# Softmax weights in five chunks of 128 rows in place of six of 122, with bias and condition moved out of the matmul

## The chip, the cores and the metric

The kernel runs on one core of a Trainium2 chip. The metric is the device time of one execution in microseconds (us), lower is better. The core's engines are TensorE (PE in the profile; its weight loads are PEld), VectorE (DVE), ScalarE (ACT), GpSimd (POOL) and SyncE (SP), which here only issues DMAs. Each runs its own instructions in order and waits on semaphores.

## The reference, cut to what matters

A graph attention layer over B=128 batches of N=128 nodes with F=512 features, H=16 heads of 32 and, in each of two directions, NONGT=20 key nodes per batch:

```
row_zero = exp_v.sum(-1) == 0
q_exp = where(row_zero, 0, q[:, None, :])                 # the condition, dropped for zero rows
self_feat = concat([exp_v, q_exp]) @ W_self.T + b_self
output = self_feat
for d in range(2):
    qh, kh = projections of self_feat and of its first 20 nodes
    aff = einsum(qh, kh) / sqrt(32), masked and biased by the edges of direction d
    w = softmax(aff, axis=-1)                             # 128 nodes x 16 heads x 20 keys
    output += einsum(w, kv, Wout[d]) + bout[d]
out = exp_v + relu(output)
```

The kernel multiplies kv by Wout[d] beforehand ("values"), so that the last einsum is, per batch, one product of the softmax weights (128 nodes x 640 pairs of direction, head and key) with a block-diagonal matrix of values. Sums of a row's weights over one head and direction are 1.

## The kernel before, in words

Three stages, each a block of its own; at a block's end all engines meet.

`prepare_weights` (lines 167 to 420) transposes and folds the weights, splits each into a high and a low part (float32r, a faster fp32 matmul form of which three make one product), and computes the condition's share of the self features (`c_dram`, one row of 512 per batch) and the bias row b_self + bout[0] + bout[1] (`bias_dram`, lines 307 to 309 and 237).

`keys_and_values` (lines 427 to 704) computes keys and values in four blocks of 32 batches. Per block come 16 halves of keys, then 16 halves of values; ACT copies each half of the values out of PSUM (line 640), DVE transposes it in 32x32 blocks (line 560) into one of four buffers `vt`, and SP stores it to `v_dram` (line 496), one DMA each: 64 in all.

`main_loop` (lines 707 to 1367) takes 32 groups of G=4 batches. PE's order is written out by hand in `group` (line 1287). In group g it computes the queries of g in eight chunks (`queries`, line 1303, 12 matmuls of 512 columns each), and between these finishes batches 1 to 3 of group g-1: `values(g-1, 1)` after chunk 0, `turn_weights(g-1, 2, ...)`, `values(g-1, 2)` after chunk 2, and so on to `values(g-1, 3)` after chunk 4. Then come self features (line 1250, 12 matmuls a batch into an output bank) mixed with the scores of the batches (line 1238), the transposes of batch 0 and its values, scores 3, the flags for the next group, and the first transposes of batch 1.

Per batch the softmax runs through the engines: scores on PE; masks and maximum on DVE (`add_masks`, line 1020); subtraction on POOL (`shift`, 913); exponentials on ACT (1154); sums and reciprocals on DVE (`denominators`, 1043); the weights `wt` on POOL (`normalise`, lines 916 to 931); transposes on PE in two parts of three chunks (`turn_weights`, 1254 to 1264); a copy of each part from PSUM to `wtt` on ACT (`weights_out`, 1156 to 1162; the second part's transposes wait for the first part's copy, line 1261); values on PE (1266 to 1277), which add to the bank of the self features; and `finish` on DVE (1051 to 1057): relu plus the kept nodes `xk` into `res`.

A chunk of `wt` holds 3 heads x 2 directions x 20 keys = 120 columns, a flag column (1 where the node's row is not zero) and a column of ones: WP=122. The sixth chunk holds one head. The matching rows of `vbd` are the block-diagonal values, the condition row and the bias row. A fp32 matmul or its weight load is two instructions in the trace, a transpose is one.

ACT's order is in its own `group` (line 1180): after the exponentials of batch 0 it makes two `row_sums` of the next group's nodes (lines 1164 to 1177; the first waits for the load of `xk`), then the exponentials of batch 1, two more row sums, then `weights_out(g, 0, 0)`.

SP's order in group g is (lines 849 to 885): rows of g+1; keys of g (`kbd`); stores of batches 1 to 3 of g-1, each waiting for its finish; the values of g (`vbd`, eight DMAs, lines 866 to 873, six of 100 rows and two of 20, 512 B a row); the condition row (line 874); the kept nodes of g+1 (line 825, 1 MB); the edges of g+1 (lines 829 and 832); the store of batch 0 of g.

Of the kernel before, what the change touches and what calls it, by code (L numbers as in the profile page):

```python
# [85 lines left out]
def build(nc, x, cond, adj, W_self, b_self, w_bias, b_bias, Wq, bq, Wk, bk, Wout, bout, out):  # L86
# [13 lines left out]
    W3 = 3  # L100
    NW = (H + W3 - 1) // W3
    WROWS = DIRS * W3 * NG
# [9 lines left out]
    v_dram = nc.dram_tensor("v_dram", [DIRS, H * Q, B, DH], F32, kind="Internal").ap()  # L112
    c_dram = nc.dram_tensor("c_dram", [B, F], F32, kind="Internal").ap()
    bias_dram = nc.dram_tensor("bias_dram", [1, F], F32, kind="Internal").ap()

    with ExitStack() as whole:
# [18 lines left out]
        bq_all = sb("bq_all", [P, DIRS * C], F32)  # L135
        identity = sb("identity", [P, P], F32)
# [30 lines left out]
def prepare_weights(nc, sb, sem, bank, v):  # L167
# [11 lines left out]
    brows = sb("brows", [1, 3, F], F32)  # L179
# [41 lines left out]
    with nc.Block() as block:  # L221
        @block.sync
        def _(sp):
            for n, src in enumerate(sources):
                if n >= 2:

                    sp.wait_ge(mat_turned, turned_before(n - 1))
                t = src.shape[0] // Q
                load_quarters(sp, stage[:, n % 2, 0:t, :], src, loaded[n % 2])
                if n == 0:  # L230
                    sp.dma_start(w1, v["Wself_x"].rearrange("(p j) f -> p j f", j=C)).then_inc(w1_loaded, 16)

            sp.wait_ge(pe_fold, DIRS * C)
            load_block_rows(sp, v, 0, kv_loaded)

            sp.wait_ge(bias_done, 2)
            sp.dma_start(v["bias_dram"], brows[:, 2, :]).then_inc(stored, 16)
            sp.wait_ge(crow_out, 1)
            sp.dma_start(v["c_dram"], crows).then_inc(stored, 16)
            sp.wait_ge(stored, 32)  # L240

            sp.wait_ge(low_done, 2 * len(SPLITS))
            sp.wait_ge(low_dve, 2 * len(SPLITS))
# [21 lines left out]
        def _(dve):  # L265
# [41 lines left out]
            nc.vector.tensor_tensor(brows[:, 1, :], brows[:, 0, :], brows[:, 1, :], ALU.add).then_inc(bias_done, 1)  # L307
            dve.wait_ge(bias_done, 1)
            nc.vector.tensor_tensor(brows[:, 2, :], brows[:, 1, :], brows[:, 2, :], ALU.add).then_inc(bias_done, 1)
# [32 lines left out]
        def _(act):  # L342

            act.wait_ge(mat_turned, turned_before(1))
            act.dma_start(brows[:, 0, :], v["b_self"].rearrange("(a f) -> a f", a=1)).then_inc(small, 16)
            act.dma_start(brows[:, 1:3, :], v["bout"].rearrange("(a d) f -> a d f", a=1)).then_inc(small, 16)
            with nc.allow_non_contiguous_dma(reason="bias vectors, one value per partition"):
                act.dma_start(cb[:, :, B:B + 1],
                              v["b_self"].rearrange("(p j a) -> p j a", j=C, a=1)).then_inc(small, 16)
                act.dma_start(bqk[:, 0, :], v["bq"].rearrange("d (c p) -> p (d c)", p=P)).then_inc(small, 16)  # L350
# [76 lines left out]
def keys_and_values(nc, sb, sem, bank, v):  # L427
# [44 lines left out]
    with nc.Block() as block:  # L472
        @block.sync
        def _(sp):
            def one_block(blk, last):
# [27 lines left out]
        def _(dve):  # L503
# [16 lines left out]
            def one_block(blk, last):  # L520
# [33 lines left out]
                for n in range(2 * NK):  # L554
# [3 lines left out]
                    if due(8 * NK * blk + 16 * (n // 4)):  # L558
                        dve.wait_ge(v_stored[n % 4], 8 * NK * blk + 16 * (n // 4))
# [45 lines left out]
        def _(act):  # L605
# [7 lines left out]
            def one_block(blk, last):  # L613
# [6 lines left out]
                for n in range(4 * NK):  # L620
# [14 lines left out]
                    else:  # L635
                        m = n - 2 * NK

                        if due(2 * NK * blk + max(m - 1, 0)):
                            act.wait_ge(v_turned, 2 * NK * blk + max(m - 1, 0))
                        nc.scalar.activation(vst[:, m % 2, :, 0:NG], src.rearrange("p (b m) -> p b m", m=NG),  # L640
                                             ACT.Copy).then_inc(kv_out, 1)
# [65 lines left out]
def main_loop(nc, sb, sem, bank, v):  # L707

    B, N, F, C, NG, L, G, GROUPS, DH, HC, W3, NW, WROWS = (v[n] for n in (
        "B", "N", "F", "C", "NG", "L", "G", "GROUPS", "DH", "HC", "W3", "NW", "WROWS"))  # L710
# [5 lines left out]
    FULL = H // W3  # L716
    WP = WROWS + 2

# [7 lines left out]
    copied = sb("copied", [P, F], F32)  # L726
    nzc = sb("nzc", [P, 2, G], BF16)
    nzb = sb("nzb", [P, 2, T], BF16)
# [4 lines left out]
    vbd = sb("vbd", [P, NW, W3, G * DH], F32)  # L733
# [5 lines left out]
    vb = sb("vb", [P, N], F32)  # L739
    cn = sb("cn", [P, N], F32)  # L740
    mk = sb("mk", [P, N], F32)
# [7 lines left out]
    wt = sb("wt", [P, 2, NW, WP], F32)  # L749
    wtt = sb("wtt", [P, 2, NW, P], F32)  # L750
    res = sb("res", [P, 2, F], F32)
# [8 lines left out]
    out_stored = [sem("out_stored0"), sem("out_stored1")]  # L760
    edge_consts = sem("edge_consts")
    bias_loaded = sem("bias_loaded")
# [24 lines left out]
    flag_ready = sem("flag_ready")  # L787
# [13 lines left out]
    def by_head(row):  # L801

        return row.rearrange("p c h (b e) -> p (c h) b e", e=DH)[:, 0:H]
# [17 lines left out]
    with nc.Block() as block:  # L821
        @block.sync
        def _(sp):
# [16 lines left out]
            for s in v["v_stored"]:  # L840
                sp.wait_ge(s, 8 * DIRS * C * v["KBLOCKS"])
            sp.wait_ge(cleared, 4)

            def store(g, b):
                sp.wait_ge(res_ready, G * g + b + 1)
                sp.dma_start(v["out"][bass.ds(g * G + b, 1)].rearrange("b n f -> (b n) f"),
                             res[:, b % 2, :]).then_inc(out_stored[b % 2], 16)

            def group(g, par, i, first, last):
# [16 lines left out]
                for d in range(DIRS):  # L866
                    vv = v["v_dram"][d].rearrange("(h m) b e -> h m b e", m=Q)[:, 0:NG, bass.ds(g * G, G), :]
                    for h in range(W3):
                        r = d * W3 * NG + h * NG
                        sp.dma_start(vbd[r:r + NG, 0:FULL, h, :],  # L870
                                     vv[h:h + W3 * (FULL - 1) + 1:W3].rearrange("c m b e -> m c (b e)")).then_inc(vbd_loaded, 16)
                    r = d * W3 * NG
                    sp.dma_start(vbd[r:r + NG, FULL, 0, :], vv[W3 * FULL].rearrange("m b e -> m (b e)")).then_inc(vbd_loaded, 16)
                sp.dma_start(by_head(vbd[WROWS:WROWS + 1]),
                             v["c_dram"][bass.ds(g * G, G)].rearrange("(a b) (h e) -> a h b e", a=1, e=DH)).then_inc(vbd_loaded, 16)
# [12 lines left out]
            for s in out_stored:  # L888
                sp.wait_ge(s, 32 * GROUPS)

        @block.gpsimd
        def _(pool):
# [10 lines left out]
            for s in v["k_stored"]:  # L903
                pool.wait_ge(s, 16 * DIRS * C * v["KBLOCKS"])
            for s in v["v_stored"]:
                pool.wait_ge(s, 8 * DIRS * C * v["KBLOCKS"])
            pool.memset(wt[:, :, :, 0:WP - 1], 0.0).then_inc(cleared, 1)
            pool.memset(wt[:, :, :, WP - 1:WP], 1.0).then_inc(cleared, 1)
# [7 lines left out]
            def normalise(g, b):  # L916
# [4 lines left out]
                for d in range(DIRS):  # L921
                    e = sc[:, b % 2, d * HM:d * HM + FULL * W3 * NG].rearrange("p (c h m) -> p c h m", h=W3, m=NG)
                    r = rs[:, b % 2, d * H:d * H + FULL * W3].rearrange("p (c h) -> p c h", h=W3)
                    o = wt[:, b % 2, 0:FULL, d * W3 * NG:(d + 1) * W3 * NG].rearrange("p c (h m) -> p c h m", m=NG)
                    pool.tensor_tensor(o, e, r.unsqueeze(3).to_broadcast([P, FULL, W3, NG]),  # L925
                                       ALU.mult).then_inc(wt_ready, 1)

                e = sc[:, b % 2, :].rearrange("p (d h m) -> p d h m", d=DIRS, m=NG)[:, :, H - 1, :]
                r = rs[:, b % 2, :].rearrange("p (d h) -> p d h", d=DIRS)[:, :, H - 1:H]
                o = wt[:, b % 2, FULL, 0:WROWS].rearrange("p (d m) -> p d m", d=DIRS)[:, :, 0:NG]  # L930
                pool.tensor_tensor(o, e, r.to_broadcast([P, DIRS, NG]), ALU.mult).then_inc(wt_ready, 1)
# [34 lines left out]
        def _(dve):  # L966
# [7 lines left out]
            def nonzero_rows(g, par):  # L974
                dve.wait_ge(summed, G * g + G)
                nc.vector.tensor_scalar(nzc[:, par, :], sums[:], 0.0, None, ALU.not_equal).then_inc(nzc_ready, 1)
# [43 lines left out]
            def add_masks(g, par, b):  # L1020
# [3 lines left out]
                if due(3 * (G * g + max(b - 1, 0))):  # L1024
                    dve.wait_ge(wt_ready, 3 * (G * g + max(b - 1, 0)))
# [3 lines left out]
                for d, (s, m) in enumerate(((S0, m0), (S1, m1))):  # L1029
                    nc.vector.tensor_tensor(  # L1030
                        sc[:, b % 2, d * HM:d * HM + HM].rearrange("p (h m) -> p h m", m=NG),
# [5 lines left out]

                if due(G * g + max(b - 1, 0)):
                    dve.wait_ge(pe_tb, G * g + max(b - 1, 0))
# [11 lines left out]
            def finish(g, par, b, last=False):  # L1051

                dve.wait_ge(pe_out, G * g + b + 1)
                if due(32 * g + 16 * (b // 2)):
                    dve.wait_ge(out_stored[b % 2], 32 * g + 16 * (b // 2))
                nc.vector.scalar_tensor_tensor(out=res[:, b % 2, :], in0=out_bank(b, last)[:], scalar=0.0,  # L1056
# [8 lines left out]
            def group(g, par, i, first, last):  # L1065
# [39 lines left out]
                if first:  # L1105
                    nonzero_rows(0, 0)
                    dve.wait_ge(cleared, 4)
# [26 lines left out]
        def _(act):  # L1134
            act.dma_start(wb[:], v["w_bias"].partition_broadcast(P)).then_inc(edge_consts, 16)
            act.dma_start(bb[:], v["b_bias"].partition_broadcast(P)).then_inc(edge_consts, 16)
            act.wait_ge(cleared, 4)
            for b in range(G):

                act.dma_start(by_head(vbd[WROWS + 1:WROWS + 2])[:, :, b, :],  # L1140
                              v["bias_dram"].rearrange("a (h e) -> a h e", e=DH)).then_inc(bias_loaded, 16)

# [13 lines left out]
            def weights_out(g, b, part, last=False):  # L1156

                if due(G * g + max(b - 1, 0)):
                    act.wait_ge(pe_out, G * g + max(b - 1, 0))
                act.wait_ge((pe_ta, pe_tb)[part], G * g + b + 1)  # L1160
                nc.scalar.activation(wtt[0:WP, b % 2, 3 * part:3 * part + 3, :], turn_bank(part, last)[0:WP, 0:3 * P],  # L1161
                                     ACT.Copy).then_inc(wtt_ready, 1)

            def row_sums(g, par, i, batches):

                if batches[0] == 0:
                    act.wait_ge(xk_loaded[par], 16 * i + 16)

                    if due(g):
                        act.wait_ge(nzc_ready, g)  # L1170
# [220 lines left out]
```

## Time and profile before

| | us |
|---|---|
| median of 3 runs | 1987.47 (1986.26 to 1987.71) |
| span of the profiled execution, its own time | 1984.9 |
| PE busy | 1950.9 (98%), 11272 instructions |
| DVE / POOL / ACT busy | 1307.5 (66%) / 880.8 (44%) / 504.4 (25%) |
| DMA | 193.87 MB, mean 98 GB/s |

The profiled execution is told by its span, from the first to the last instruction; the runs' times are taken without a profile and hold a little more than the span. A line such as L1275 is a line of the kernel before. Matmuls overlap, so PE's busy time says that work is there, not that it runs at its best; the chain of work that ended last says what the time hangs on.

### The profile page before, as it was taken

The page shows a single profiled execution, that of the slowest core. Times are in us where ns is not written, and L with a number is a line of the kernel's source. Part 1 is how long each engine was busy: PE and PEld are TensorE (multiplying, and loading weights), DVE is VectorE, ACT ScalarE, POOL GpSimd, SP SyncE. Part 2 cuts the span into 40 slices and gives each one's busy share as a digit, 9 for nine tenths or more (in the row PEclk, how much of TensorE's full clock was granted, in tenths as well). Part 3 has the DMA queues.
Part 4 walks back from the last instruction along what each step waited for, and adds up shares of the span by engine and source line. Part 5 has one row for each costly group of instructions (what it writes and reads, how often), then busy time and mean ns, then how long its engine had stood idle before and what let it go on. Part 6 is the DMA issues. An engine that isn't in the chain of part 4 may idle for free.

```text
span 1984.9 us, 33656 instructions
## 1 busy us (share of the span) xinstructions
PE 1950.9 (98%) x11272; PEld 1703.3 (86%) x11272; DVE 1307.5 (66%) x1866; ACT 504.4 (25%) x1022; POOL 880.8 (44%) x981
## 2 busy tenths in 40 slices
PE   5899999999999999999999999999999999999999
PEld 3899999988888888888888888888888888888888
DVE  6623223277777777777777777777777777777775
ACT  2231221322222222222222222222222222222221
POOL 1412132145554445554455555555555544444453
PEclk9999999999999999999999999999999999999999
DMA  9523323253333333333333334343434333333321
GB/s 168 87 91 88 134 70 106 107 146 96 96 96 95 95 95 95 95 97 98 95 98 97 99 95 98 96 99 94 98 96 98 96 98 95 98 98 95 95 75 39
DMA packets 234210, 193.87 MB, mean 98 GB/s; under 512 B 52275, under 2 KB 190003, under 8 KB 234166
## 3 DMA queue, kind: packets, MB, share of 16 engines
q1 hardware_dynamic: 231138, 193.26, 38.6%
q10 hardware_dynamic: 3028, 0.03, 0.1%
q8 instruction: 27, 0.44, 0.1%
q14 instruction: 17, 0.14, 0.0%
HBM read 132.15 MB, written 61.08 MB: 97 GB/s over the span
## 4 chain that ended last, share of the span: by engine, by line
PE 79%; DVE 0%; ACTq 0%; issue 0%; ACT 0%
PE bank L1303 36%; PE bank L1250 18%; PE bank L1238 12%; PE bank L1275 8%; PE bank L1263 5%; PE bank L1223 0%; PE bank L1283 0%; PE bank L1312 0%; DVE res L1056 0%; ACTq L821 0%; ACT wtt L1161 0%; ACTq L1160 0%
## 5 line engine op out<-in xcount | busy, mean ns | idle before, releaser
L942 POOL TENSOR_TENSOR rc<-nzb,cqg 128x512 f32<-128x512 bf16 x256 | 265.4, 1042 | 450.4 <-DVE qt_main L1069 450.2
L1069 DVE SCALAR_TENSOR_TENSOR qt_main<-bank,bq_all,rc 128x512 f32<-128x512 f32 x256 | 189.4, 740 | 191.0 <-PE bank L1303 187.5
L1238 PEld LDWEIGHTS bank<-kbd,qt_main 128*128 128x128 f32 x2048 | 241.6, 192 | 16.1 <-issue 7.6
L1238 PE MATMUL bank<-kbd,qt_main 128*128 128x80 f32 x2048 | 249.4, 275 | 0.0
L913 POOL TENSOR_TENSOR sc<-sc,mx 128x640 f32<-128x640 f32 x128 | 163.3, 1276 | 181.4 <-DVE mx L1035 180.5
L1161 ACT ACTIVATE wtt<-bank 122x384 f32<-122x384 f32 x256 | 124.9, 489 | 446.6 <-PE bank L1263 446.6
L1303 PE MATMUL bank<-xh_odd,wq_h 128*128 128x512 f32 x512 | 210.1, 410 | 0.0
L1303 PE MATMUL bank<-nodes_h,wq_h 128*128 128x512 f32 x512 | 209.7, 410 | 0.0
L925 POOL TENSOR_TENSOR wt<-sc,rs 128x300 f32<-128x300 f32 x256 | 172.9, 697 | 69.2 <-DVE rs L1049 67.1
L1303 PE MATMUL bank<-nodes_l,wq_h 128*128 128x512 f32 x512 | 201.9, 394 | 0.0
L1303 PE MATMUL bank<-xl_odd,wq_h 128*128 128x512 f32 x512 | 201.9, 394 | 0.0
L1303 PE MATMUL bank<-nodes_h,wq_l 128*128 128x512 f32 x512 | 201.8, 394 | 0.0
L1303 PE MATMUL bank<-xh_odd,wq_l 128*128 128x512 f32 x512 | 201.8, 394 | 0.0
L1275 PEld LDWEIGHTS bank<-vbd,wtt 122*128 122x128 f32 x1536 | 191.2, 192 | 11.3 <-ACT wtt L1161 0.9
L1275 PE MATMUL bank<-vbd,wtt 122*128 122x96 f32 (+1 forms) x1536 | 182.1, 268 | 0.7 <-ACT wtt L1161 0.7
L1030 DVE TENSOR_TENSOR sc<-bank,m 128x320 f32<-128x320 f32 x256 | 111.6, 478 | 96.8 <-PE bank L1238 96.8
L664 PE MATMUL bank<-kv_fh,wkv_h 128*128 128x320 f32 x512 | 157.4, 308 | 0.0
L664 PE MATMUL bank<-kv_fl,wkv_h 128*128 128x320 f32 x512 | 157.4, 308 | 0.0
L664 PE MATMUL bank<-kv_fh,wkv_l 128*128 128x320 f32 x512 | 157.4, 307 | 0.0
L83 DVE STREAM_TRANSPOSE nodes_t<-rows 128x512 f32<-128x512 f32 (+1 forms) x144 | 156.3, 1108 | 0.0
L1154 ACT ACTIVATE sc<-sc 128x640 f32<-128x640 f32 x128 | 94.6, 739 | 239.2 <-POOL sc L913 239.2
L560 DVE STREAM_TRANSPOSE kv_vt<-kv_vst 128x512 f32<-128x512 f32 x64 | 45.5, 711 | 162.4 <-ACT kv_vst L640 162.4
(120 smaller groups left out, 3920.0 us busy)
## 6 DMA issues: line engine op xcount, KB each, us to landing
rows<-in_x SPq DMA_DIRECT2D x128, 256.0 KB, 4.9
xk<-in_x SPq DMA_DIRECT2D x32, 1024.0 KB, 5.4
out<-res SPq DMA_DIRECT2D x128, 256.0 KB, 2.1
v_dram<-kv_vt SPq DMA_DIRECT2D x64, 256.0 KB, 2.0
adj<-in_mask_BxSxSx_ik SPq DMA_DIRECT2D x32, 440.0 KB, 6.3
adj<-in_mask_BxSxSx_ik SPq DMA_DIRECT2D x128, 110.0 KB
k_dram<-kv_kst SPq DMA_DIRECT2D x64, 160.0 KB, 1.8
kbd<-k_dram SPq DMA_DIRECT2D x128, 80.0 KB, 5.6
```

The costliest lines, as they stand in the source:

```text
L83: return eng.transpose(dst, src.rearrange("p t (r j) -> p t r j", j=NQ)[:, :, :, j])
L664: mm = nc.tensor.matmul(dst, a(j), b(j), start=(j == 0 and k == 0), stop=(j == C - 1 and k == 2))
L913: pool.tensor_tensor(s, s, mx[:, b % 2, :].unsqueeze(2).to_broadcast([P, DIRS * H, NG]), ALU.subtract).then_inc(s_shifted, 1)
L925: pool.tensor_tensor(o, e, r.unsqueeze(3).to_broadcast([P, FULL, W3, NG]), ALU.mult).then_inc(wt_ready, 1)
L942: pool.tensor_tensor(rc[:, c % 2, :].rearrange("p (b n) -> p b n", b=G), nzb[:, par, :].rearrange("p (b n) -> p b n", b=G), cqg[:, par, c, ...
L1030: nc.vector.tensor_tensor(sc[:, b % 2, d * HM:d * HM + HM].rearrange("p (h m) -> p h m", m=NG), s[:, 0:HM].rearrange("p (h m) -> p h m", m ...
L1069: nc.vector.scalar_tensor_tensor(out=qt[:, c, :], in0=bank[c % 2][:], scalar=bq_all[:, c:c + 1], in1=rc[:, c % 2, :], op0=ALU.add, op1=ALU ...
L1161: nc.scalar.activation(wtt[0:WP, b % 2, 3 * part:3 * part + 3, :], turn_bank(part, last)[0:WP, 0:3 * P], ACT.Copy).then_inc(wtt_ready, 1)
L1238: mm = nc.tensor.matmul(dst, qt[:, c, b * N:b * N + N], kbd[:, c, :, b * NG:b * NG + NG], start=True, stop=True)
L1250: mm = nc.tensor.matmul(out_bank(b, last)[:], a, m[:, j, :], start=(j == 0 and k == 0), stop=False)
L1275: mm = nc.tensor.matmul(out_bank(b, last)[:, c * W3 * DH:(c * W3 + heads) * DH], wtt[0:WP, b % 2, c, :], vbd[0:WP, c, 0:heads, b * DH:b * ...
L1303: mm = nc.tensor.matmul(bank[c % 2][:], a, m, start=(j == 0 and k == 0), stop=(j == C - 1 and k == 2))
```

## The change

The weights of all 640 (head, direction, key) columns are laid out head first, without gaps, and cut into five chunks of 128. A chunk then begins and ends within a head, so its values matmul covers four heads (128 output columns) in place of three (96), and `vbd` is loaded in 20 pieces. The bias is added to the values of direction 0 when ACT copies them out of PSUM in the second stage (the weights of a head sum to 1). The condition is loaded into `res`, one copy of the group's four rows in each of 128 partitions, multiplied on ACT by the flag of the node, and added on DVE at the output. `res` holds four batches in place of two. Stores of values in the second stage are one per head.

```diff
@@ keys_and_values, SP
-                        sp.dma_start(v["v_dram"][d, c * P:c * P + P, bass.ds(blk * KB + h * HB, HB), :],
-                                     vt[:, n % 4]).then_inc(v_stored[n % 4], 16)
+                        for k in range(NQ):
+                            sp.dma_start(v["v_dram"][NQ * c + k, d, :, bass.ds(blk * KB + h * HB, HB), :],
+                                         vt[Q * k:Q * k + NG, n % 4]).then_inc(v_stored[n % 4], 16)
@@ keys_and_values, ACT
+                        if m < 2 * C:
+                            nc.scalar.activation(o, src.rearrange("p (b m) -> p b m", m=NG), ACT.Identity,
+                                                 bias=v["v_bias"][:, m // 2:m // 2 + 1]).then_inc(kv_out, 1)
@@ main_loop
+    def value_pieces():
+
+        for c in range(NW):
+            for s in range(SLOTS):
+                h = 3 * c + s
+                yield c, s, max(P * c, WH * h), min(P * c + P, WH * h + WH)
@@ main_loop, SP
+            def load_condition(g):
+
+                if due(64 * g):
+                    sp.wait_ge(out_stored, 64 * g)
+                sp.dma_start(res[:].rearrange("p b f -> p (b f)"),
+                             v["c_dram"][bass.ds(g * G, G)].rearrange("(a b) f -> a (b f)", a=1)
+                             .to_broadcast([P, G * F])).then_inc(c_loaded, 16)
...
-                for d in range(DIRS):
-                    vv = v["v_dram"][d].rearrange("(h m) b e -> h m b e", m=Q)[:, 0:NG, bass.ds(g * G, G), :]
-                    for h in range(W3):
...
+                vv = v["v_dram"].rearrange("h d m b e -> (h d m) b e")[:, bass.ds(g * G, G), :]
+                for c, s, lo, hi in value_pieces():
+                    sp.dma_start(vbd[lo - P * c:hi - P * c, c, s, :],
+                                 vv[lo:hi].rearrange("r b e -> r (b e)")).then_inc(vbd_loaded, 16)
+                load_condition(g)
                 if not last:
 
                     load_kept(g + 1, 1 - par)
@@ main_loop, POOL normalise: three products become one
+                e = sc[:, b % 2, :].rearrange("p (h m) -> p h m", m=NG)
+                o = wt[:, b % 2, :].rearrange("p (h m) -> p h m", m=NG)
+                pool.tensor_tensor(o, e, rs[:, b % 2, :].unsqueeze(2).to_broadcast([P, DIRS * H, NG]),
+                                   ALU.mult).then_inc(wt_ready, 1)
@@ main_loop, DVE
-                nc.vector.tensor_copy(wt[:, b % 2, :, WROWS:WROWS + 1].rearrange("p c a -> p (c a)"),
-                                      nzc[:, par, b:b + 1].to_broadcast([P, NW])).then_inc(flag_ready, 1)
...
-                nc.vector.scalar_tensor_tensor(out=res[:, b % 2, :], in0=out_bank(b, last)[:], scalar=0.0,
+                n = G * g + b
+                dve.wait_ge(c_scaled, n + 1)
+                dve.wait_ge(pe_out, n + 1)
+                nc.vector.tensor_tensor(res[:, b, :], out_bank(b, last)[:], res[:, b, :], ALU.add).then_inc(out_taken, 1)
+                dve.wait_ge(out_taken, n + 1)
+                nc.vector.scalar_tensor_tensor(out=res[:, b, :], in0=res[:, b, :], scalar=0.0,
                                                in1=xk[:, par, b, :], op0=ALU.max, op1=ALU.add).then_inc(res_ready, 1)
@@ main_loop, ACT
+            def scale_condition(g, par, b):
+
+                if b == 0:
+                    act.wait_ge(c_loaded, 16 * g + 16)
+                    act.wait_ge(nzc_ready, 2 * g + 2)
+                nc.scalar.activation(res[:, b, :], res[:, b, :], ACT.Copy,
+                                     scale=nzf[:, par, b:b + 1]).then_inc(c_scaled, 1)
...
                 weights_out(g, 0, 0, last)
                 weights_out(g, 0, 1, last)
+                scale_condition(g, par, 0)
                 exponentials(g, 2)
+                scale_condition(g, par, 1)
                 if not last:
                     flags(g + 1, 1 - par)
                 weights_out(g, 1, 0, last)
+                scale_condition(g, par, 2)
@@ main_loop, PE; PARTS = ((0, 3), (3, 5))
-                        pe.wait_ge(res_ready, G * g + (1 if b == 3 else 0))
+                        pe.wait_ge(out_taken, G * g + (1 if b == 3 else 0))
...
-                for c in range(3):
+                lo, hi = PARTS[part]
+                for c in range(lo, hi):
...
-                    heads = W3 if c < FULL else H - FULL * W3
-                    mm = nc.tensor.matmul(out_bank(b, last)[:, c * W3 * DH:(c * W3 + heads) * DH], wtt[0:WP, b % 2, c, :],
-                                          vbd[0:WP, c, 0:heads, b * DH:b * DH + DH], start=False, stop=(c == NW - 1))
+                    mm = nc.tensor.matmul(out_bank(b, last)[:, 3 * c * DH:(3 * c + SLOTS) * DH], wtt[:, b % 2, c, :],
+                                          vbd[:, c, :, b * DH:b * DH + DH], start=False, stop=(c == NW - 1))
```

## Rows read from the trace of the kernel before

**Rows 1.** The page: busy times and granted clock.
```profile
PE 1950.9 (98%) x11272; PEld 1703.3 (86%) x11272; DVE 1307.5 (66%) x1866; ACT 504.4 (25%) x1022; POOL 880.8 (44%) x981
...
PEclk9999999999999999999999999999999999999999
```

**Rows 2.** The page: the chain that ended last, by line.
```profile
PE bank L1303 36%; PE bank L1250 18%; PE bank L1238 12%; PE bank L1275 8%; PE bank L1263 5%; PE bank L1223 0%; PE bank L1283 0%; PE bank L1312 0%; DVE res L1056 0%; ACTq L821 0%; ACT wtt L1161 0%; ACTq L1160 0%
```

**Rows 3.** The chain, in order of time, one group: start us, us, what.
```profile
1009.18 2.78 PE bank L1303 x12
1011.96 1.26 PE bank L1275 x12
1013.22 8.48 PE bank L1303 x36
...
1033.57 0.33 PE bank L1263 x3
...
1034.60 0.49 PE bank L1263 x3
...
1062.32 2.88 PE bank L1303 x12
```

**Rows 4.** Timeline of PE, preparation: start us, us, engine, line, op, shapes, count.
```profile
64.80 7.31 PE L418 MATMUL bank<-cb,wqt 128*128 128x129 f32 x64
```

**Rows 5.** Timeline of POOL, one batch's weights.
```profile
1031.35 1.35 POOL L925 TENSOR_TENSOR wt<-sc,rs 128x300 f32<-128x300 f32 x2
```

**Rows 6.** Timeline of DVE, the finish of batch 3.
```profile
1016.81 0.68 DVE L1056 SCALAR_TENSOR_TENSOR res<-bank,xk 128x512 f32<-128x512 f32 x1
```

**Rows 7.** Timeline of ACT, with idle before and what ended it.
```profile
1028.43 0.74 ACT L1154 ACTIVATE sc<-sc 128x640 f32<-128x640 f32 x1 [3.79 <-POOL sc L913]
1029.07 0.62 ACT L1176 ACTIVATE copied<-xk 128x512 f32<-128x512 f32 x1
...
1031.43 0.74 ACT L1154 ACTIVATE sc<-sc 128x640 f32<-128x640 f32 x1 [0.89 <-POOL sc L913]
...
1034.00 0.49 ACT L1161 ACTIVATE wtt<-bank 122x384 f32<-122x384 f32 x1 [0.46 <-PE bank L1263]
```

**Rows 8.** Timeline of SP's issues in the same group.
```profile
1017.66 0.33 SPq L846 DMA_DIRECT2D out<-res  x1
1018.18 1.31 SPq L870 DMA_DIRECT2D vbd<-v_dram  x3
1019.67 0.30 SPq L873 DMA_DIRECT2D vbd<-v_dram  x1
1020.15 1.23 SPq L870 DMA_DIRECT2D vbd<-v_dram  x3
...
1022.04 0.61 SPq L874 DMA_DIRECT2D vbd<-c_dram  x1
1022.75 0.54 SPq L825 DMA_DIRECT2D xk<-in_x  x1
```

**Rows 9.** The page: DMA issues, KB each, us to landing.
```profile
xk<-in_x SPq DMA_DIRECT2D x32, 1024.0 KB, 5.4
```

**Rows 10.** Windows: stretch, us, busy of PE, PEld, DVE, ACT, POOL; PEclk, DMA share, GB/s.
```profile
1025.00:1027.00 2.00, 2.00 (x14) 1.65 (x13) 1.67 (x4) 0.00 (x0) 0.00 (x0) 1.00 0.98 374
1029.00:1031.00 2.00, 2.00 (x11) 1.60 (x10) 1.93 (x5) 1.51 (x5) 0.88 (x1) 1.00 0.63 127
72.20:78.10 5.90, 0.00 (x0) 0.00 (x0) 4.83 (x18) 1.46 (x2) 2.85 (x2) 0.79 0.00 0
78.20:82.40 4.20, 4.20 (x16) 4.20 (x17) 1.49 (x3) 0.00 (x0) 0.80 (x1) 0.50 0.79 155
404.60:406.50 1.90, 0.00 (x0) 0.00 (x0) 0.71 (x1) 0.41 (x1) 0.00 (x0) 1.00 0.37 138
406.60:410.00 3.40, 3.40 (x9) 2.62 (x10) 2.19 (x1) 0.00 (x0) 3.40 (x2) 0.52 0.63 182
```

**Rows 11.** Timeline of SP, stores of values, last block.
```profile
381.15 24.97 SPq L496 DMA_DIRECT2D v_dram<-kv_vt  x15
```

More of the change, by code:

```diff
@@ L707, in main_loop @@
 def main_loop(nc, sb, sem, bank, v):
[L709 to L710 removed]
+    B, N, F, C, NG, L, G, GROUPS, DH, HC, WH, NW = (v[n] for n in (
+        "B", "N", "F", "C", "NG", "L", "G", "GROUPS", "DH", "HC", "WH", "NW"))
     ws_h, ws_l, wq_h, wq_l, cq, bq_all = (v[n] for n in ("ws_h", "ws_l", "wq_h", "wq_l", "cq", "bq_all"))
@@ L715, in main_loop @@
     NC = DIRS * C
-    FULL = H // W3
-    WP = WROWS + 2
+    SLOTS = 4
+    PARTS = ((0, 3), (3, 5))
+    assert H * WH == NW * P and NW == 5
     rows = v["rows"][:, 0:T // Q]
@@ L725, in main_loop @@
     sums = sb("sums", [P, G], F32)
-    copied = sb("copied", [P, F], F32)
+    copied = v["rows"][:, T // Q:, :].rearrange("p t k -> p (t k)")
     nzc = sb("nzc", [P, 2, G], BF16)
+    nzf = sb("nzf", [P, 2, G], F32)
     nzb = sb("nzb", [P, 2, T], BF16)
@@ L738, in main_loop @@
     bb = sb("bb", [P, 1], F32)
-    vb = sb("vb", [P, N], F32)
-    cn = sb("cn", [P, N], F32)
-    mk = sb("mk", [P, N], F32)
+    vb, cn, mk = (v["nodes_t"][:, j, T:] for j in range(3))
     m0 = sb("m0", [P, G, NG], F32)
@@ L887, in _ @@
             groups(sp, group)
-            for s in out_stored:
-                sp.wait_ge(s, 32 * GROUPS)
+            sp.wait_ge(out_stored, 64 * GROUPS)
         @block.gpsimd
@@ L975, in nonzero_rows @@
                 dve.wait_ge(summed, G * g + G)
+                nc.vector.tensor_scalar(nzf[:, par, :], sums[:], 0.0, None, ALU.not_equal).then_inc(nzc_ready, 1)
                 nc.vector.tensor_scalar(nzc[:, par, :], sums[:], 0.0, None, ALU.not_equal).then_inc(nzc_ready, 1)
@@ L1160, in weights_out @@
                 act.wait_ge((pe_ta, pe_tb)[part], G * g + b + 1)
-                nc.scalar.activation(wtt[0:WP, b % 2, 3 * part:3 * part + 3, :], turn_bank(part, last)[0:WP, 0:3 * P],
-                                     ACT.Copy).then_inc(wtt_ready, 1)
+                lo, hi = PARTS[part]
+                nc.scalar.activation(wtt[:, b % 2, lo:hi, :].rearrange("p c t -> p (c t)"),
+                                     turn_bank(part, last)[:, 0:(hi - lo) * P], ACT.Copy).then_inc(wtt_ready, 1)
+            def scale_condition(g, par, b):
[4 more added lines that the diff above has]
+                                     scale=nzf[:, par, b:b + 1]).then_inc(c_scaled, 1)
             def row_sums(g, par, i, batches):
@@ L1175, in row_sums @@
                             act.wait_ge(summed, G * g + b)
-                    nc.scalar.activation(copied[:], xk[:, par, b, :], ACT.Copy,
+                    nc.scalar.activation(copied, xk[:, par, b, :], ACT.Copy,
                                          accum_out=sums[:, b:b + 1]).then_inc(summed, 1)
@@ L1256, in turn_weights @@
                 n = G * g + b
-                pe.wait_ge(wt_ready, 3 * n + 3)
-                pe.wait_ge(flag_ready, n + 1)
+                pe.wait_ge(wt_ready, n + 1)
                 if due(2 * n + (0 if last else part)):
                     pe.wait_ge(wtt_ready, 2 * n + (0 if last else part))
-                for c in range(3):
-                    mm = nc.tensor.transpose(turn_bank(part, last)[0:WP, c * P:c * P + P], wt[:, b % 2, 3 * part + c, :], identity[:])
+                lo, hi = PARTS[part]
+                for c in range(lo, hi):
+                    mm = nc.tensor.transpose(turn_bank(part, last)[:, (c - lo) * P:(c - lo) * P + P],
+                                             wt[:, b % 2, c * P:c * P + P], identity[:])
                 mm.then_inc((pe_ta, pe_tb)[part], 1)
```

104 lines of the change are left out of this document (36 added, 68 removed).

## The prediction

> **What bounds the kernel now.** I read the page's busy times first, then its chain, then the chain of one group in order of time, then each queue of that group.
>
> PE is busy for 98% of the span at a granted clock of nine tenths or more, and of the engines beside it none is above 66% [rows 1]. Busy PE alone proves little, so the chain decides: 79% of the span lies on it as matmuls of the main loop [rows 2]. In order of time, the first queries after values of group 19 begin at 1013.22 us and those of group 20 at 1062.32 us: a period of 49.10 us per group of four batches [rows 3]. The only wait of PE in it is a small one: the second set of three transposes takes 0.49 us where the first takes 0.33. So whatever shortens PE's stream pays in full, and whatever makes PE wait costs in full.
>
> **What PE gains.** Transposes: three cost 0.33 us, 0.11 each [rows 3]; one of six goes, 0.11 us a batch. The first part keeps three, only the second has two. Values: each fp32 matmul is two instructions. Now 6x2 of 96 or 32 columns take 1.26 us up to the end of the last, and the 512-column queries behind them begin their steady rhythm 0.1 us late [rows 3], about 1.34 us or 0.112 us an instruction. Afterwards there are 5x2 of 128 columns. No values instruction has 128 columns before, but the nearest row does: 64 instructions of 129 columns took 7.31 us up to the end of the last, so at most 0.114 us each, and 0.112 to 0.113 without its tail [rows 4]. Ninety-six and 129 columns cost the same, so the price is the weight load, and the columns ride along. I take 10x0.112 = 1.12, a gain of 0.22 (bounds: 0.14 if I compare with 1.26; nothing or a loss if columns are the price, below). Together 0.33 us a batch, 128 batches: -42.7 us.
>
> The Trainium skill, page "TensorE: Matmul & The Clock Gate", section "Back-to-back issue gap", speaks against this: a matmul's gap is N/2.4 + 2.5 ns, so 128 columns cost more than 96. By that rule the five wider matmuls would be dearer than the six, not cheaper. The 129-column row says otherwise, where a weight load stands before each matmul.
>
> **What the other engines get.** POOL makes the same 640 products in one instruction instead of 300+300+40 (1.35 us for the two large ones) [rows 5]: no dearer. DVE loses four small casts a group and gains one addition of 512 per batch beside its present 0.68 us finish [rows 6]: 4x0.68 less the casts, on an engine at 66%; hidden, except that each finish ends 0.68 us later. Who waits for that: the store, below. PE's wait for an output bank moves to the addition's end, as early as before. ACT gains four scalings of 512, near 0.6 us like the row sums [rows 7], on an engine at 25%; they stand behind the weights' copy of batch 0 and ahead of later exponentials, whose results PE needs only microseconds later. If that cover is gone they cost 0.6 us each. The bias moves into an ACT copy that existed: nothing.
>
> **SP's queue is where it turns.** In each group SP issues, after the store of batch 3, eight loads of values and one condition row, then the load of the next group's nodes (1 MB). The eight begin at 1018.18 and the condition at 1022.04: 0.483 us each, whether a DMA moves 100 rows or 20 (1.49 us for three of 100 rows, 0.48 for one of 20). The node load is issued at 1022.75 [rows 8]. It lands 5.4 us later [rows 9], at 1028.15; ACT begins its row sums at 1029.07 [rows 7]. Slack there: 0.92 us.
>
> After the change SP issues 20 value loads there, and the condition load becomes 1 MB (2,048 values into each of 128 partitions) and stands ahead of the nodes. Step by step:
> - the store starts 0.68 us later (two-step finish);
> - 20x0.483 = 9.66 in place of 3.86: +5.80;
> - the condition's issue keeps its 0.71; its wait for all stores is over by then (the last store is issued 10 us before);
> - so the node load is issued at 1022.75+6.48 = 1029.23, and alone would land at 1034.6;
> - ahead of it in the DMA rings is the condition's 1 MB: at the 374 GB/s of the present node load [rows 10] 2.8 us, less the 0.7 between the issues: +2.1. It lands at 1036.7. Bounds: +0, if the two share without loss; +7.5, if 8 KB rows move at the 127 GB/s of the large-row edge loads [rows 10].
>
> ACT works in order. From that landing it does two row sums (1.5 us), the exponentials of batch 1 (0.65), two row sums (1.5), then copies the transposed weights of batch 0 (0.49): 4.15-4.2 us, so that copy ends at 1040.9 where now it ends at 1034.49 [rows 7]. PE's second transposes of batch 0 wait for exactly this copy [rows 3]. PE stalls 6.4 us (bounds 4.3 and 11.8). Behind PE in that wait are the rest of self features 2, values 0, scores 3: all of the group. Nothing absorbs it later, since PE has no idle time, and the anchor of the next group (the finish of batch 3) is moved along with PE, so it recurs. The first group issues its loads early and the last loads no nodes: 30 groups, 30x6.4 = +192 us.
>
> **The clock.** PE had nothing to do for 5.9 us before 78.2, and the granted clock was then 0.50 (the lower level, 1.2 GHz) for 4.2 us of work: 2.1 us lost. After the 2 us gap at 404.6 it was 0.52 over 3.4 us: 1.7 us lost [rows 10]. I take 1.8 per stall: +54 us. Bounds: 0 and 2.1.
>
> The same page of the Trainium skill, in its section "The HAM clock gate (the \"warmup\" mystery)", holds that idleness throttles PE to 1.2 GHz and activity releases it; the two rows agree.
>
> **Keys and values.** The 64 stores become 256. Now the stores of a block follow DVE's transposes, one per 1.76 us (15 in 24.97 us) [rows 11]. Four issues at 0.483 take 1.93 us, so SP falls back 0.17 a step, 2.8 us over 16, and the last four take 1.9 where one took 0.5. Inside a block a ring of four buffers covers that; at the end all engines meet before the main loop: about +4.1 us, once (bounds: 1.4 if nothing piles up, 5.2 at the 0.497 us of the slowest three issues). Preparation loses SP's bias store and gains two small scattered loads: nothing within 1 us. At the very end the two-step finish adds 0.68.
>
> **Sum.** The profiled span is 1984.9 us; -42.7, +4.1, +0.7, +192, +54 gives 2193. The median of the runs, 1987.47, lies 2.6 above the span: **2195 us**.
>
> **Rivals.**
> 1. Faster: the node load stays hidden and only PE's gain shows: 1984.9-42.7+4.8+2.6 = **1950 us**. The place is SP's issue of the 20 value loads. The delay fits if 0.68+20p-3.86 stays within 0.92 plus ACT's idle 0.89 and 0.46 [rows 7], so if p is below 0.27 us and the condition's 1 MB costs nothing. For it: ACT, DVE and DMA (about 40% used) have room on average. Against: the eight issues keep a mean of 0.483 us, and 20 rows cost as much as 100 [rows 8]. 0.06.
> 2. The stall comes, the clock stays up: 2195-54 = **2141 us**. Against it stand both rows of the clock. 0.12.
> 3. The broadcast is slow: stall 11.8, **2357 us**. For it: the large-row edge loads reach only 127 GB/s; against: those use few partitions, this one all 128. 0.09.
> 4. Columns are the price of a values matmul. Twelve 512-column matmuls take 2.78 us [rows 3], 0.45 ns a column; 256 more columns a batch would add 0.12 us instead of saving 0.22: 0.34x128 = +43, **2238 us**. This is how the page's gap rule would come out here; the 129-column row is against it. 0.04.
> 5. Stall and gain nearly cancel (a stall of 1.2 us): 0.02.
>
> The forecast itself has 0.67; its own spread is 2145 to 2250 (stall 5 to 8 with the clock's part). The 8-in-10 range takes in rivals 2 and 4 and part of the bounds: 2100 to 2280. A measurement of this kernel tells about 0.2% from no change; by the cases: faster 0.07, same 0.02, slower 0.91.
>
> **What would show it.** In the new profile: a period near 55-57 us; values as 10 instructions in about 1.1 us; 20 value issues on SP over 9 to 10 us; ACT's first row sum waiting on the DMA of the nodes, 28 to 30 times, 6 us or more each; PE (or its weight load) waiting on ACT's copy before the second transposes of batch 0; granted clock below 1 in every slice of the main loop. The prediction is wrong if SP's issues are much shorter, if ACT's wait is on something else or absent, or if PE's stream did not shrink.

## The result, and the profile after

| | before | after |
|---|---|---|
| median of the runs, us | 1987.58 (4 runs) | 2196.69 (2194.3 to 2198.73, 4 runs) |
| span of the profiled execution, us | 1984.9 | 2194.4 |

The ratio is 1.105, 95% interval 1.104 to 1.107: slower. The forecast was 2195 us.

The page of the changed kernel: busy times, granted clock, the chain, and the transfers of nodes and condition (KB each, us to landing).

```profile
PE 1979.8 (90%) x10888; PEld 1722.9 (79%) x10888; DVE 1323.7 (60%) x1898; ACT 567.5 (26%) x1150; POOL 841.8 (38%) x723
...
PE 48%; SPq 11%; DMA 10%; issue 6%; ACT 4%; DVE 2%; ACTq 0%; DVEq 0%
PE bank L1305 25%; DMA xk<-in_x 10%; SPq L884 10%; PE bank L1253 8%; PE bank L1277 7%; PE bank L1266 3%; PE bank L1241 3%; ACT rows L1174 3%; DVE res L1051 1%; DVE res L1049 1%; ACT sc L1143 1%; SPq L856 1%; SPq L862 1%; ACT wtt L1151 1%; PE bank L1226 0%
...
xk<-in_x SPq DMA_DIRECT2D x32, 1024.0 KB, 7.4
res<-c_dram SPq DMA_DIRECT2D x32, 1024.0 KB, 4.6
```

Before, the chain was PE and nothing else that counts [rows 2]. Now a quarter of it is SP's issues of the value loads (L884), the landing of the nodes and the work that hangs on it. PE's share of the span fell from 98% to 90% [rows 1], though it has 384 instructions fewer.

The chain in order of time through one group (start us, us, what) shows the road:

```profile
1151.04 0.69 DVE res L1049
1151.76 1.04 DVE res L1051
...
1163.63 7.34 DMA xk<-in_x
...
1171.08 0.73 ACT rows L1174 x2
1171.83 0.72 ACT rows L1174 x2
1172.55 0.63 ACT sc L1143
1173.18 0.62 ACT rows L1174 x2
...
1174.55 0.39 ACT wtt L1151
...
1174.98 0.69 PE bank L1266 x2
...
1187.68 1.12 PE bank L1277 x10
...
1191.92 0.22 PE bank L1266 x2
```

DVE makes the finish of batch 3 in its two steps; behind its store SP issues the 20 value loads, the condition, then the nodes (the queue is below); the nodes land at 1170.97; ACT does two row sums, an exponential and two row sums, and only then the copy that PE's second transposes wait for. Beside it stand the gains: ten values instructions in 1.12 us where twelve took 1.26, two transposes in 0.22 where three took 0.33 [rows 3].

SP's queue over that group, then ACT and PE at the wait (idle before, and what ended it):

```profile
1152.95 0.33 SPq L862 DMA_DIRECT2D out<-res  x1
1153.46 9.47 SPq L884 DMA_DIRECT2D vbd<-v_dram  x20
1163.18 0.36 SPq L856 DMA_DIRECT2D res<-c_dram  x1
1163.63 0.40 SPq L833 DMA_DIRECT2D xk<-in_x  x1
```

```profile
1171.08 0.63 ACT L1174 ACTIVATE rows<-xk 128x512 f32<-128x512 f32 x1 [7.23 <-DMA xk<-in_x]
```

```profile
1174.98 0.69 PE L1266 MATMUL bank<-identity,wt 128*128 128x128 f32 x2 [5.50 <-ACT wtt L1151]
```

Twenty value loads take 9.72 us, 0.486 each, where eight took 3.86 [rows 8]. ACT idles 7.2 us, PE 5.5. Summed over the run, the waits (us in total, times, longest) are:

```profile
ACT rows L1174 <- DMA xk<-in_x: 227.7, 31, 10.4
PE bank L1266 <- ACT wtt L1151: 165.7, 30, 6.3
PE bank L1241 <- DVE qt_main L1064: 14.0, 30, 0.8
```

The 30 groups are there, with 5.5 us each. The third row is a wait that the prediction does not have: PE waits 0.47 us for DVE before the first scores of each group. The windows of the wait, of the work behind it, and of one whole group (columns as in [rows 10]):

```profile
1169.30:1174.90 5.60, 0.17 (x1) 0.00 (x0) 1.65 (x4) 3.76 (x10) 0.40 (x1) 0.72 0.71 226
1175.00:1178.90 3.90, 3.90 (x14) 3.32 (x15) 1.93 (x6) 2.34 (x4) 3.29 (x3) 0.54 0.00 0
1150.60:1206.23 55.63, 49.63 (x274) 42.10 (x273) 36.58 (x54) 14.49 (x30) 23.43 (x20) 0.94 0.38 103
```

The granted clock is 0.54 over the 3.9 us behind the wait, so the lower level (1.2 GHz) nearly throughout. The period is 55.63 us, against 49.10.

### The profile page after: what moved, and what is told of

It reads as the page before. It is cut to its first block, busy times and chain, and to the rows that moved or that the text cites. A ratio compares the mean times of both kernels' runs of the same rounds, so it can differ in the third digit from the quotient of the medians.

```text
span 2194.4 us, 34072 instructions
## 1 busy us (share of the span) xinstructions
PE 1979.8 (90%) x10888; PEld 1722.9 (79%) x10888; DVE 1323.7 (60%) x1898; ACT 567.5 (26%) x1150; POOL 841.8 (38%) x723
## 3 DMA queue, kind: packets, MB, share of 16 engines
q1 hardware_dynamic: 236256, 220.28, 37.9%
## 4 chain that ended last, share of the span: by engine, by line
PE 48%; SPq 11%; DMA 10%; issue 6%; ACT 4%; DVE 2%; ACTq 0%; DVEq 0%
PE bank L1305 25%; DMA xk<-in_x 10%; SPq L884 10%; PE bank L1253 8%; PE bank L1277 7%; PE bank L1266 3%; PE bank L1241 3%; ACT rows L1174 3%; DVE res L1051 1%; DVE res L1049 1%; ACT sc L1143 1%; SPq L856 1%; SPq L862 1%; ACT wtt L1151 1%; PE bank L1226 0%
## 5 line engine op out<-in xcount | busy, mean ns | idle before, releaser
L1039 DVE TENSOR_REDUCE sm<-sc 128x32 f32<-128x640 f32 x128 | 104.6, 817 | 347.5 <-ACT sc L1143 347.5
L1241 PEld LDWEIGHTS bank<-kbd,qt_main 128*128 128x128 f32 x2048 | 249.2, 195 | 33.2 <-issue 25.5
L1266 PE MATMUL bank<-identity,wt 128*128 128x128 f32 x640 | 120.1, 288 | 165.7 <-ACT wtt L1151 165.7
L927 POOL TENSOR_TENSOR wt<-sc,rs 128x640 f32<-128x640 f32 x128 | 162.8, 1272 | 247.0 <-DVE rs L1042 245.4
L1266 PEld LDWEIGHTS bank<-identity,wt 128*128 128x128 f32 x640 | 81.3, 146 | 195.9 <-ACT wtt L1151 170.9
L1151 ACT ACTIVATE wtt<-bank 128x384 f32<-128x384 f32 (+1 forms) x256 | 110.7, 433 | 399.2 <-PE bank L1266 399.1
L1277 PEld LDWEIGHTS bank<-vbd,wtt 128*128 128x128 f32 x1280 | 184.1, 213 | 14.8 <-ACT wtt L1151 1.3
L1277 PE MATMUL bank<-vbd,wtt 128*128 128x128 f32 x1280 | 182.7, 295 | 0.7 <-ACT wtt L1151 0.7
```

The costliest lines, as they stand in the source:

```text
L927: pool.tensor_tensor(o, e, rs[:, b % 2, :].unsqueeze(2).to_broadcast([P, DIRS * H, NG]), ALU.mult).then_inc(wt_ready, 1)
L1151: nc.scalar.activation(wtt[:, b % 2, lo:hi, :].rearrange("p c t -> p (c t)"), turn_bank(part, last)[:, 0:(hi - lo) * P], ACT.Copy).then_in ...
L1241: mm = nc.tensor.matmul(dst, qt[:, c, b * N:b * N + N], kbd[:, c, :, b * NG:b * NG + NG], start=True, stop=True)
L1266: mm = nc.tensor.transpose(turn_bank(part, last)[:, (c - lo) * P:(c - lo) * P + P], wt[:, b % 2, c * P:c * P + P], identity[:])
L1277: mm = nc.tensor.matmul(out_bank(b, last)[:, 3 * c * DH:(3 * c + SLOTS) * DH], wtt[:, b % 2, c, :], vbd[:, c, :, b * DH:b * DH + DH], star ...
```

## The experiments

Theory A: the nodes come late because of what SP issues ahead of them, and ACT, in order, passes that on to PE. Rival B: the new work on ACT and DVE slows the softmax's way, and the order of the loads is beside the point. e1 to e4 ran on one chip and e5 to e8 on another; the kernel before took 1987.92 us on the first and 1987.01 us on the second, and each ratio is taken against its own.

**e1, nodes first.** SP's load of the next nodes ahead of the value loads:

```diff
+                if not last:
+                    load_kept(g + 1, 1 - par)
                 if due(G * g):
                     sp.wait_ge(pe_out, G * g)
...
                 load_condition(g)
                 if not last:
-                    load_kept(g + 1, 1 - par)
                     sp.wait_ge(m_done, 2 * g + 2)
```

> The changed kernel with one move: SP issues the load of the next group's nodes ahead of the 20 value loads and the condition load. Theory A (the nodes come late because of what SP issues before them, and ACT, in order, holds up the copy that PE waits for): ACT's wait for the nodes and PE's 5.5 us wait per group vanish, the clock stays up, and the time falls by 30 x (5.5 + about 2) to 1955 to 1975 us. Rival B (the scalings on ACT and the two-step finish on DVE slow the softmax's way, the order of loads is beside the point): it stays within 20 us of 2197.

Measured: 1968.81 us, 0.990 of the kernel before (0.989 to 0.992). The waits of this kernel:

```profile
PE bank L1242 <- DVE qt_main L1065: 14.6, 30, 0.7
...
PEld bank L1267 <- ACT wtt L1152: 10.6, 28, 0.4
```

Its SP queue:

```profile
1014.55 0.41 SPq L833 DMA_DIRECT2D xk<-in_x  x1
1015.14 9.46 SPq L887 DMA_DIRECT2D vbd<-v_dram  x20
1024.86 0.36 SPq L856 DMA_DIRECT2D res<-c_dram  x1
```

The same 20 loads and the same megabyte are issued, in as long a time; only what ACT needs first goes first. Nearly 228 us come back. ACT's wait for the nodes is gone in steady state (10.7 us, once, are left of 227.7); what is left before the second transposes (10.6 us of PEld, 28 times) is the small wait that the kernel before has (10.5 us, 28 times). Rival B is out for these 228 us. Whether the new work on ACT and DVE costs anything of what is left is asked by e5 and e8.

**e2, nodes between values and condition.** The two last loads exchanged:

```diff
+                if not last:
+                    load_kept(g + 1, 1 - par)
                 load_condition(g)
                 if not last:
-                    load_kept(g + 1, 1 - par)
                     sp.wait_ge(m_done, 2 * g + 2)
```

> The changed kernel with the nodes' load after the 20 value loads but ahead of the 1 MB condition load. Theory A: the nodes are issued 0.45 us earlier and land in about 5.4 us rather than 7.4, so PE's wait per group goes from 5.5 to about 3.1 us, and some of the clock's loss with it: 2095 to 2125 us. Rival B: within 20 us of 2197. If it falls to 1970, it was the condition's transfer alone and not the number of issues.

Measured: 2093.02 us, 1.053 (1.050 to 1.056), 2 us under the band. PE's wait:

```profile
PE bank L1266 <- ACT wtt L1151: 86.2, 30, 4.3
```

2.9 us a group in place of 5.5; the nodes land in 5.4 us in place of 7.4. So 2.6 us of the stall come from the condition's issue and its megabyte, and the rest from what still stands ahead of the nodes: the 20 value loads (e4 tests them alone) and a finish of batch 3 that ends later. Both count.

**e3, PE's wait filled.** Work that is used for nothing, into a bank that is free then:

```diff
                 self_features(g, par, 2, range(1, 2))
+                if not first and not last:
+                    for k in range(22):
+                        nc.tensor.matmul(bank[1][:], xh[par][:, k % C, 2 * N:2 * N + N], ws_h[:, k % C, :],
+                                         start=True, stop=True)
                 turn_weights(g, 0, 1, last)
```

> The changed kernel with 22 more 512-column matmuls of PE per group, placed where it waits, into a free bank and used for nothing (22 x 0.232 = 5.1 us, against a wait of 5.5). If the drop of the granted clock after the wait costs time, PE now hardly idles, the clock stays near 1.00 and the time falls although work is added: by about 1.9 us a group to 2130 to 2150 us. If the clock is only a label, it stays at 2197 or rises.

Measured: 2135.29 us, 1.074 (1.072 to 1.077): 61 us less than the changed kernel, with 660 more matmuls. The fill and what follows it (timeline of PE), and the windows of both:

```profile
1034.90 5.29 PE L1347 MATMUL bank<-ws_h,xh_odd 128*128 128x512 f32 x22
...
1040.53 0.44 PE L1266 MATMUL bank<-identity,wt 128*128 128x128 f32 x2 [0.33 <-ACT wtt L1151]
```

```profile
1034.90:1041.00 6.10, 5.77 (x26) 4.42 (x25) 2.17 (x5) 3.79 (x10) 0.95 (x1) 1.00 0.65 206
1041.00:1045.00 4.00, 4.00 (x32) 3.73 (x31) 2.03 (x7) 2.35 (x4) 2.85 (x3) 1.00 0.00 0
```

The nodes come no earlier: ACT waits for them as long as in the changed kernel:

```profile
ACT rows L1174 <- DMA xk<-in_x: 227.4, 31, 10.6
```

So the copy that PE needs comes no earlier either. But the granted clock is 1.00 in both stretches. The drop of the clock alone costs 61/30 = 2.05 us a group.

**e4, the kernel before with 20 value loads.** Nothing of the change but the count of issues (and, with it, the count of landings that PE waits for, 336 a group in place of 144):

```diff
-                        sp.dma_start(vbd[r:r + NG, 0:FULL, h, :],
-                                     vv[h:h + W3 * (FULL - 1) + 1:W3].rearrange("c m b e -> m c (b e)")).then_inc(vbd_loaded, 16)
+                        for c0, c1 in ((0, 2), (2, 4), (4, 5)):
+                            sp.dma_start(vbd[r:r + NG, c0:c1, h, :],
+                                         vv[h + W3 * c0:h + W3 * (c1 - 1) + 1:W3].rearrange("c m b e -> m c (b e)")).then_inc(vbd_loaded, 16)
```

> The kernel before with one edit: the six 100-row value loads of a group are cut into 18 (with the two of 20 rows 20 loads, same bytes), all else as before: six chunks, no condition broadcast, no scalings. Theory A: 12 more issues of 0.48 us push the nodes' load 5.8 us back; less the slack of 0.9 + 1.35 PE waits 3.5 us a group, and the clock takes 1 to 2 more: 2120 to 2150 us. Rival B: it stays at 1987.

Measured: 2133.3 us (2125.58 and 2141.01), 1.073 (1.069 to 1.078). The queue and the waits are those of the faster one. SP's queue (x9 is half of the 18 loads; the other half and the two of 20 rows are left out) and the waits:

```profile
1127.30 4.17 SPq L871 DMA_DIRECT2D vbd<-v_dram  x9
...
1136.89 0.61 SPq L875 DMA_DIRECT2D vbd<-c_dram  x1
1137.59 0.54 SPq L825 DMA_DIRECT2D xk<-in_x  x1
```

```profile
ACT copied L1177 <- DMA xk<-in_x: 142.9, 30, 5.6
...
PE bank L1264 <- ACT wtt L1162: 96.6, 30, 4.0
```

The same bytes in 20 pieces make the old kernel 7% slower. From the first value load to the nodes' issue it is now 10.3 us, where it was 4.57 [rows 8]; PE waits 3.2 us a group, expected 3.5. This is theory A in reverse.

**e5, one transpose behind the last query chunk.** On top of e1, for the third wait:

```diff
                     turn(g + 1, 1 - par, 1)
-                    turn(g + 1, 1 - par, 2)
                 q_evacuate(7)
                 if not last:
+                    turn(g + 1, 1 - par, 2)
                     turn(g + 1, 1 - par, 3)
```

> e1_nodes_first with one DVE instruction moved: the third transpose of the next group's nodes stands behind the reading of query chunk 7 rather than ahead of it (1 us). If the 0.5 us that PE waits for chunk 7 before the first scores of each group is DVE's, late through the two-step finish, it vanishes: 30 x 0.5, from 1969 to 1951 to 1957 us. If that wait comes from elsewhere: 1969.

Measured: 1952.42 us, 0.982 (0.981 to 0.984): it beats both kernels. The chain, two groups' first queries apart:

```profile
1002.18 8.40 PE bank L1306 x36
...
1025.39 1.11 PE bank L1278 x10
...
1050.11 8.41 PE bank L1306 x36
```

A period of 47.93 us against 49.10 [rows 3]. PE's wait for chunk 7 is gone. What DVE still holds up is the weight load of a group's second scores (13.4 us of PEld in all, of PE itself 0.2), and e8 shows that this still costs some time:

```profile
PEld bank L1242 <- DVE sc L1029: 13.4, 31, 0.7
```

**e6, 96 columns.** e5 with a fourth of the columns left out of each values matmul, so head 15 and parts of four others are missing from the output:

```diff
-                    ...[:, 3 * c * DH:(3 * c + SLOTS) * DH], wtt[:, b % 2, c, :],
-                                          vbd[:, c, :, b * DH:b * DH + DH]
+                    ...[:, 3 * c * DH:(3 * c + 3) * DH], wtt[:, b % 2, c, :],
+                                          vbd[:, c, 0:3, b * DH:b * DH + DH]
```

> e5_turn_late with 96 in place of 128 columns in each of the five values matmuls (the fourth head of a chunk is left out of the product, so head 15 and parts of four others are missing). If the weight load is the price of a values instruction: the same time as e5 within 4 us. If columns are: 320 fewer column passes a batch at 0.45 ns, 0.145 us x 128 = 18 us less.

Measured: 1951.87 us (1949.91 to 1952.41), 0.55 less than e5. In its chain ten values instructions take

```profile
1001.15 1.09 PE bank L1278 x10
```

against 1.11 with 128 columns in e5. So the columns are not the price; it is paid per instruction, 0.11 us, and each of these has a weight load of its own. That it is the weight load, and not something else in the instruction, no run here separates.

**e7, the kernel before with nodes first.** The edit of e1 on the old kernel.

> The kernel before with the nodes' load ahead of its eight value loads. Its nodes came in time already, so theory A expects no change: 1985 to 1990 us. Were it faster, part of what e1 gained would be the order's own and not the smaller product's.

Measured: 1987.52 us, 1.000 (0.999 to 1.001). Nothing of the gain of e1 and e5 is the order's own.

**e8, finish in one step.** e1 without the addition of the condition (it is loaded and scaled, and left out of the output). PE's wait for an output bank goes back to the finish:

```diff
-                nc.vector.tensor_tensor(res[:, b, :], out_bank(b, last)[:], res[:, b, :], ALU.add).then_inc(out_taken, 1)
-                dve.wait_ge(out_taken, n + 1)
-                nc.vector.scalar_tensor_tensor(out=res[:, b, :], in0=res[:, b, :], scalar=0.0,
+                nc.vector.scalar_tensor_tensor(out=res[:, b, :], in0=out_bank(b, last)[:], scalar=0.0,
...
-                        pe.wait_ge(out_taken, G * g + (1 if b == 3 else 0))
+                        pe.wait_ge(res_ready, G * g + (1 if b == 3 else 0))
```

> e1_nodes_first with the finish in one DVE step again (the condition is loaded and scaled, but not added to the output). If the two-step finish is what delays DVE, PE's 0.5 us wait per group before the first scores goes, as in e5: 1951 to 1957 us; the ACT scalings and the 1 MB load stay and cost nothing. If those cost something, it stays above 1960.

Measured: 1946.95 us, 0.980 (0.978 to 0.981), 4 us below the band. PE waits for no DVE result in the main loop's steady state now, so it was the finish; going back to one step gives 5 us more than e5's moved transpose, with the rest of DVE's hold-up. The chain, from the values of one group's batch 0 to those of the next:

```profile
1022.69 1.11 PE bank L1276 x10
...
1070.48 1.11 PE bank L1276 x10
```

A period of 47.79 us (the mean of all groups is the same), 1.31 less than before [rows 3], where 1.33 was forecast for PE's stream. The scalings on ACT and the megabyte of condition are still there: they cost nothing that these runs can tell. So of rival B one part is true and small: the finish on DVE, 21.9 us from e8 to e1.

## Why the prediction was right

Mechanism, place, number of groups and time were as forecast, and the experiments undo and redo it. The total is closer (2195 against 2196.7) than the terms deserve, and that part is luck: the stall was put 26 us too high, and a cost forecast as nothing, 22 us, made up for it, with a clock's loss that was 7 us larger. From measured differences:

| term | forecast | measured |
|---|---|---|
| PE's gain, with the start of the main loop and the tail | -42.7 + 4.8 = -37.9 | -40.1 (before to e8, 1987.0 to 1946.95) |
| DVE's longer finish | 0 | +21.9 (e8 to e1) |
| PE's wait for the nodes, 30 groups | +192 | +165.7 (the waits' row) |
| lower clock behind it | +54 | +61.4 (after to e3) |

The measured terms, added to 1987.0, give 2195.9. The first two lead from the kernel before to e1 by the way they are measured, so their sum proves nothing. The test is in the last two: together 227.1 us, against 227.9 measured from e1 to the changed kernel. The kernels of a row did not all run on one chip, and the time of the kernel before differs by up to 0.9 us between the chips, so each of these differences is good to about 1 us.

**PE's gain** is right: the period of e8 is 1.31 us shorter, and 1.33 was forecast. (That of e5 is 1.17 shorter, since DVE still holds PE up there.) That columns ride along, read off the 129-column row [rows 4], holds (e6). The forecast set the Trainium skill against itself here with half of what it says. In "TensorE: Matmul & The Clock Gate", section "Back-to-back issue gap", the formula N/2.4 + 2.5 ns is that of an isolated matmul; in a stream where each matmul has its weight load, the section says, both set the spacing, and the formula comes out too small for few columns. e6 agrees with the section as a whole: 96 columns and 128 take the same time, 1951.87 and 1952.42 us.

**The nodes' delay**: +6.48 us to the issue was forecast. From the start of the finish of batch 3 (1016.81 before [rows 6], 1151.04 in the chain) to the nodes' issue it went from 5.94 to 12.59, so +6.65. Here too errors cancel: the store came 1.06 us later and not 0.68, the value loads took 5.86 more, and the condition's issue 0.45 in place of 0.71. Landing took 7.34 us, forecast 5.4 + 2.1 = 7.5. The rival of the slow broadcast is out: the condition lands in 4.6 us.

**The stall** was mis-sized, 5.5 in place of 6.4. Two reasons stand in the traces: PE itself came 0.6 us later to the place of the wait (its last product ahead of it starts 18.71 us behind DVE's reading of chunk 5, before 18.07), most of it by its new wait for DVE, and ACT needed 3.95 us from landing to the copy's end (1170.97 to 1174.92) where I took 4.15 to 4.2.

**DVE's finish** is the step that failed: "hidden, except that each finish ends 0.68 us later", so nothing in the sum; it cost 21.9 us. I named the store as the only one who waits for that. Behind the finish on DVE also stood a transpose, the reading of chunk 6, two transposes and the reading of chunk 7, and PE's first scores wait for that last one. I had costed DVE by its 66% share of the span, which says nothing of the order of its queue. The second step is also longer than I took it (last section).

**The clock**: 1.8 a stall forecast, 2.05 measured by e3. The two rows of [rows 10] gave a fair price, though the second, 3.4 us at 0.52, is 1.6 us lost and not 1.7.

**Keys and values**: +4.1 forecast, and the pile-up did not come. SP's queue there, last block:

```profile
379.62 27.72 SPq L495 DMA_DIRECT2D v_dram<-kv_vt  x64
```

64 issues in 27.72 us are 0.433 each, 1.73 for four, just under the 1.76 of DVE's pace [rows 11]. The main loop's first loads are issued 1.3 us later (407.82 against 406.51 in the two SP timelines), which is about the lower bound. But PE's idle time there grew from 2.03 to 3.19 us and the clock stayed low longer. The windows 405 to 415 us, of the kernel before and then of the changed one, show 30 and 19 matmuls begun, 0.83 and 0.66 of the clock:

```profile
405.00:415.00 10.00, 8.43 (x30) 6.72 (x31) 4.26 (x4) 0.38 (x2) 7.53 (x6) 0.83 0.76 231
```

```profile
405.00:415.00 10.00, 7.12 (x19) 5.61 (x20) 5.19 (x3) 0.16 (x1) 6.43 (x4) 0.66 0.62 178
```

Eleven matmuls at 0.233 us make 2.6 us, once, where 4.1 was forecast: about half is the later start, the rest the lower clock, a term that the forecast did not have here. Its cause, a pile-up of stores, was wrong.

Of the signs that the forecast listed, the period (55 to 57), the ten values instructions, the 20 issues in 9 to 10 us, ACT's wait and PE's wait all showed. "Granted clock below 1 in every slice" held for the windows of the main loop (0.94), while the page's digits, which stop at 9, cannot show it.

## What to carry to other kernels

In these kernels an issue on SP's queue took 0.43 to 0.50 us, whether it moved 20 rows or 100, so cutting a load to fit a tidier layout is paid in the queue: count the issues, and see what stands behind them. Put the load whose user comes first in front (1968.8 against 2196.7 us for one moved line), and ask what an in-order engine has behind the instruction that waits. A shorter instruction stream on the bounding engine is only worth its price where every engine that feeds it, waits included, still comes in time.

## What the runs showed of the hardware that was not expected

The DVE finish with both inputs in SBUF takes from 0.69 to 1.32 us in the changed kernel, with the same shape. DVE's and POOL's timelines tell why:

```profile
1189.63 0.69 DVE L1051 SCALAR_TENSOR_TENSOR res<-res,xk 128x512 f32<-128x512 f32 x1
...
1199.81 0.68 DVE L1049 TENSOR_TENSOR res<-bank,res 128x512 f32<-128x512 f32 x1
1200.52 1.04 DVE L1051 SCALAR_TENSOR_TENSOR res<-res,xk 128x512 f32<-128x512 f32 x1
```

```profile
1188.55 1.04 POOL L939 TENSOR_TENSOR rc<-nzb,cqg 128x512 f32<-128x512 bf16 x1 [0.64 <-DVE qt_main L1064]
...
1199.97 1.04 POOL L939 TENSOR_TENSOR rc<-nzb,cqg 128x512 f32<-128x512 bf16 x1 [3.17 <-DVE qt_main L1064]
```

At 1189.63 POOL has just ended its product; at 1200.52 it works until 1201.01, and the finish takes 0.35 us more. The addition just ahead of it, with one input in PSUM, overlaps the same POOL product and keeps its 0.68 us, as the old finish had [rows 6]. All 128 finishes follow this: the 46 that overlap a POOL instruction by 0.10 us or less take 0.69 us, the 62 that overlap one by 0.48 to 0.50 take 1.03 or 1.04, the three that overlap by 0.77 or 0.78 take 1.32. So a finish loses the overlap less about 0.14 us. None of the 128 additions is longer than 0.69, with up to 0.74 us of overlap. The Trainium skill, page "SBUF — State Buffer", section "Who interferes with whom", states that a DVE instruction with two SBUF inputs contends with a GpSimd instruction that reads SBUF, and one with at most one SBUF input, outside DVE's 2-port modes, does not; these rows agree. I had not applied it to the second step of the finish.

The other is how cheap idle-time work is: 22 useless matmuls a group made the kernel 61 us faster, because the granted clock stayed at 1.00.
